# Fourier transforms of folded images in a convolution, attention and expert kernel

## The reference

```
# 1. a 7x7 depthwise convolution whose filters are computed from the image itself
g = group_norm(x)
key = softmax(K_w @ g + K_b)                  # over the 256 positions, 49 keys
filters = relu(norm(conv0_w @ (g @ key) + conv0_b) * ln_w + ln_b)
x = x + depthwise_conv(g, conv1_w @ filters + conv1_b, padding=3)
# 2. attention over the 256 positions, as tokens of 128 features
z = norm(x);  q = tanh(z);  x = x + softmax(q q^T / sqrt(128)) z
# 3. 8 experts, the best 2 for each token
z = norm(x);  p, i = top2(softmax(z @ router_w + router_b))
x = x + sum_k p_k * expert_{i_k}(z)
```

## Time and profile before

| | us |
|---|---|
| runs, median (of 3) | 386.15 (382.89 to 387.73) |
| profiled execution | 386.41 |
| its span | 384.6 |
| TensorE busy in it | 302.8 |
| VectorE busy in it | 236.7 |
| ScalarE busy in it | 132.4 |
| GpSimd busy in it | 164.2 |

### The profile page before, as it was taken

The page is one execution under the profiler, slowest core; times in us unless marked ns, Lnnn a source line. Parts: engine busy times, 40 slices in busy tenths (PEclk is TensorE's granted clock), DMA queues, the critical chain, the costliest instruction groups (busy, mean ns, idle before and its releaser), DMA issues.

```text
span 384.6 us, 7449 instructions
## 1 busy us (share of the span) xinstructions
PE 302.8 (79%) x1731; PEld 239.7 (62%) x1732; DVE 236.7 (62%) x1006; ACT 132.4 (34%) x443; POOL 164.2 (43%) x187
## 2 busy tenths in 40 slices
PE   1686989998989899998876661599999999999200
PEld 1264667786868777777664440388878787888100
DVE  2433475488887877676866652266666676666164
ACT  0312221425152515141303012266656565666000
POOL 3000010030256565555455577046656566666400
PEclk9958896999999999989887655599999999999755
DMA  7722241221523000101010013223332322231197
GB/s 221 250 80 67 84 125 28 85 68 30 182 79 97 31 30 21 38 21 37 22 35 29 29 56 107 55 80 81 85 94 84 89 77 83 80 93 59 48 322 288
DMA packets 29945, 33.37 MB, mean 87 GB/s; under 512 B 5096, under 2 KB 23740, under 8 KB 29658
## 3 DMA queue, kind: packets, MB, share of 16 engines
q1 hardware_dynamic: 23312, 22.00, 18.9%
q0 software_dynamic: 4384, 8.60, 6.7%
q10 hardware_dynamic: 2218, 2.42, 1.8%
HBM read 21.76 MB, written 11.75 MB: 87 GB/s over the span
## 4 chain that ended last, share of the span: by engine, by line
PE 44%; issue 21%; POOL 21%; DMA 5%; DVE 4%; SPq 3%; ACT 1%; POOLq 0%; DVEq 0%; ACTq 0%
POOL rows_dram L410 15%; PE bank L1324 8%; PE bank L1312 5%; PE bank L1307 5%; PE bank L1308 5%; PE bank L1317 4%; PE bank L833 3%; DMA w_high<-moe_dram 2%; PE bank L876 2%; POOL ln_rstd L437 2%; PE bank L1302 2%; SPq L1160 2%; PE bank L978 2%; POOL ln_rstd L433 2%; PE bank L914 1%
## 5 line engine op out<-in xcount | busy, mean ns | idle before, releaser
L1132 POOL DMA_INDIRECT moe_dram<-ys,xs x72 | 70.4, 978 | 51.2 <-issue 30.8
L410 POOL DMA_INDIRECT rows_dram<-row,slot x64 | 62.7, 979 | 18.2 <-issue 18.2
L1324 PE MATMUL bank<-w_all,gatedt 128*128 x288 | 44.1, 276 | 0.2 <-ACT gatedt L1175 0.2
L1249 DVE SCALAR_TENSOR_TENSOR ys<-b_all,xs,bank 128x128 f32<-128x128 f32 x72 | 25.0, 347 | 28.5 <-issue 27.0
L1259 DVE SCALAR_TENSOR_TENSOR gated<-bank,xs,silu 128x256 f32<-128x256 f32 x72 | 34.8, 483 | 10.2 <-ACT silu L1183 7.8
L1183 ACT ACTIVATE silu<-bank 128x256 f32<-128x256 f32 x72 | 27.6, 383 | 35.7 <-PE bank L1312 35.7
L1324 PEld LDWEIGHTS bank<-w_all,gatedt 128*128 128x128 f32 x288 | 38.0, 192 | 0.4 <-issue 0.4
L1307 PE MATMUL bank<-w_high,x_high 128*128 x72 | 35.6, 494 | 0.0
L978 PE MATMUL bank<-zhat,const 121*128 121x256 f32 (+1 forms) x128 | 31.2, 399 | 0.0
L1312 PE MATMUL bank<-w_high,x_low 128*128 x72 | 30.3, 421 | 0.7 <-issue 0.7
L423 POOL TENSOR_TENSOR frstd<-fvar,minus_half 128x2 f32<-128x2 f32 x8 | 5.7, 708 | 57.5 <-DVE fvar L703 57.5
(11 more groups left out here) (172 smaller groups left out, 593.7 us busy)
## 6 DMA issues: line engine op xcount, KB each, us to landing
xs<-rows_dram SPq DMA_DIRECT2D x72, 66.0 KB, 1.8
xc<-in_x SPq DMA_DIRECT2D x8, 256.0 KB, 2.9
wgv<-in_wg SPq DMA_DIRECT2D x8, 256.0 KB, 2.9
wgv<-in_wv SPq DMA_DIRECT2D x8, 256.0 KB, 3.4
xt<-in_xt SPq DMA_DIRECT2D x4, 512.0 KB, 4.6
xt<-moe_dram SPq DMA_DIRECT2D x8, 256.0 KB, 6.0
w_high<-moe_dram SPq DMA_DIRECT2D x8, 256.0 KB, 6.6
out<-w_high ACTq DMA_DIRECT2D x8, 256.0 KB, 5.6
```

The source lines that it names most:

```text
L410: pool.indirect_dma_start(rows_dram, bass.IndirectOffsetOnAxis(ap=slot[:, f % 2, 2 * t + k:2 * t + k + 1], axis=0), row[:, f % 2, t, k, :] ...
L1132: pool.indirect_dma_start(moe_dram, bass.IndirectOffsetOnAxis(ap=xs[:, u, C + 1:C + 2].bitcast(U32), axis=0), ys[:, u, :], None, bounds_ch ...
L1324: last = pe.matmul(bank_y[v][:, 0:C], gatedt[:, v, h * P:(h + 1) * P], w2_all[:, bass.ds(e * (2 * C) + h * C, C)], start=(h == 0), stop=(h ...
```

## The change

With the centre of the image as origin, the real part of a position's wave is the same at the position opposite (turned by half a turn, position 255 - n), and the imaginary part has the other sign. So the real parts of the spectrum need only the sum of an image's two halves, chunk 1 read backwards, and the imaginary parts only the difference. The change does this both ways:

- gfold holds the sum and the difference of chunk 0 and mirrored chunk 1 of gbuf; the transposes L890 take it. The forward transform has 4 products in place of 6 (one each for r = 0 and 1, two for r = 2).
- The product of image and key probabilities runs over positions, so kprob is folded too (and halved), into kfold.
- The inverse gives an even and an odd part: 4 products in place of 8. VectorE adds both to chunk 0's residual, and to chunk 1's the even part with + and the odd with -: three instructions in place of L746.
- Chunk 1 of each pair's tokens is therefore held backwards from here on. Its tokens come by an indirect DMA on GpSimd (`mirror_rows`, a table of indices `mirror`), one for each pair, in rounds 1 to 8, and SyncE loads only chunk 0. The output of chunk 1 is scattered by GpSimd in the same way; ScalarE stores chunk 0 only.
- filt, the filters before their transform, has 128 rows with zeros below row 49 and not 49 rows. The constants are shorter (fwd 732 to 490 columns, inv 1024 to 512).

```diff
@@ constants, fwd and inv @@
+    half = np.arange(P)
+    centre = (SIDE_IN - 1) / 2
+    angle = 2 * np.pi / SIDE * (np.outer(half // SIDE_IN - centre, u) + np.outer(half % SIDE_IN - centre, v))
...
+    fwd = np.concatenate([re[:, :WIDE], im[:, :WIDE], both(re, none), both(none, im)], 1)
...
-    inv = np.zeros((P, 4, HW))
+    inv = np.zeros((P, 4, P))
@@ SyncE @@
-                        sp.dma_start(xt[:, 2 * p - 4:2 * p - 2], a_in["xt"][:, 2 * p - 4:2 * p - 2]).then_inc(ld_xt[p % 2], 16)
+                        pairs = slice(2 * p - 4, 2 * p - 2)
+                        sp.dma_start(xt[:, pairs, 0:2], a_in["xt"][:, pairs, 0:2]).then_inc(ld_xt[p % 2], 16)
@@ GpSimd @@
+                pool.memset(filt[:, :, :], 0.0).then_inc(iota_ready, 1)
...
+                pool.iota(mirror[:, :], pattern=[[CHUNKS, PAIRS]], base=(P - 1) * PAIRS * CHUNKS + 1,
+                          channel_multiplier=-PAIRS * CHUNKS).then_inc(iota_ready, 1)
...
+                mirror_rows = a_in["xt"].rearrange("p b (h s) c -> (p b h) (s c)", h=CHUNKS)
                 for i in range(rounds):
                     n, a, b, c, d, e, f = stages(i)
+                    if a is not None:
+
+                        after(pool, ld_xm[a % 2], 16 * (a // 2))
+                        pool.indirect_dma_start(xt[:, a, 2:4, :].rearrange("p s c -> p (s c)"), None, mirror_rows,
+                                                bass.IndirectOffsetOnAxis(ap=mirror[:, a:a + 1], axis=0)).then_inc(ld_xm[a % 2], 16)
                     if f is not None:
@@ VectorE @@
                         dve.wait_ge(krec_done, a + 1)
+
+                        dve.tensor_scalar(kprob[:, :], kexp[:, :], krec[:, 0:1], 0.5, ALU.mult, ALU.mult).then_inc(kprob_done, 1)
+                        dve.wait_ge(kprob_done, a + 1)
                         after(dve, pt_psum, a)
-                        dve.tensor_scalar(kprob[:, :], kexp[:, :], krec[:, 0:1], None, ALU.mult).then_inc(kprob_done, 1)
+                        dve.tensor_tensor(kfold[:, 0, :], kprob[:, 0:P], kprob[:, HW - 1:P - 1:-1], ALU.add)
+                        dve.tensor_tensor(kfold[:, 1, :], kprob[:, 0:P], kprob[:, HW - 1:P - 1:-1], ALU.subtract).then_inc(kfold_done, 1)
...
+                        dve.wait_ge(ld_xm[c % 2], 16 * (c // 2 + 1))
+                        halves = t1[:, c % 2, :, :].rearrange("p (h s) c -> p h (s c)", h=CHUNKS)
+                        dve.tensor_tensor(halves, spread(bank_o[:, 0:2 * C], 1, CHUNKS),
+                                          xt[:, c, :, :].rearrange("p (h s) c -> p h (s c)", h=CHUNKS), ALU.add).then_inc(t1_step, 1)
+                        dve.wait_ge(t1_step, c + 1)
+                        dve.tensor_tensor(halves[:, 0, :], halves[:, 0, :], bank_o[:, 2 * C:4 * C], ALU.add)
+                        dve.tensor_tensor(halves[:, 1, :], halves[:, 1, :], bank_o[:, 2 * C:4 * C], ALU.subtract).then_inc(t1_done, 1)
...
+                        dve.wait_ge(g_done, n + 1)
+                        after(dve, gt_psum, n)
+                        near = gbuf[:, n % 2, :].rearrange("p (s n) -> p s n", s=2)[:, :, 0:P]
+                        far = gbuf[:, n % 2, :].rearrange("p (s n) -> p s n", s=2)[:, :, HW - 1:P - 1:-1]
+                        dve.tensor_tensor(gfold[:, 0, :, :], near, far, ALU.add)
+                        dve.tensor_tensor(gfold[:, 1, :, :], near, far, ALU.subtract).then_inc(gfold_done, 1)
@@ TensorE @@
-                        for h in range(CHUNKS):
+                        parts = ((r, r),) if r < 2 else ((2, 0), (3, 1))
+                        for q, h in parts:
                             last = pe.matmul(bank_s[r // 2][0:tile_rows[r], r % 2 * 2 * C:(r % 2 + 1) * 2 * C],
-                                             fwd[:, h, tile_cols[r]], gt[:, b % 2, h, :],
-                                             start=(h == 0), stop=(h == CHUNKS - 1))
+                                             fwd[:, tile_cols[q]], gt[:, b % 2, h, :],
+                                             start=(q == parts[0][0]), stop=(q == parts[-1][0]))
...
-                                             tapf[0:KK, tile_cols[r]], filt[:, :, :].rearrange("k s c -> k (s c)"),
+                                             tapf[:, tile_cols[r]], filt[:, :, :].rearrange("k s c -> k (s c)"),
...
                         for h in range(CHUNKS):
-                            for r in range(4):
-                                last = pe.matmul(bank_o[:, h * 2 * C:(h + 1) * 2 * C], inv[0:tile_rows[r], r, h * P:(h + 1) * P],
-                                                 zhat[0:tile_rows[r], r, :], start=(r == 0), stop=(r == 3))
+                            for r in (h, h + 2):
+                                last = pe.matmul(bank_o[:, h * 2 * C:(h + 1) * 2 * C], inv[0:tile_rows[r], r, :],
+                                                 zhat[0:tile_rows[r], r, :], start=(r < 2), stop=(r >= 2))
@@ the end: GpSimd and ScalarE @@
+        out_rows = out.rearrange("p b (h s) c -> (p b h) (s c)", h=CHUNKS)
+        for p in range(PAIRS):
+            pool.wait_ge(S["sum_done"], p + 1)
+            pool.indirect_dma_start(out_rows, bass.IndirectOffsetOnAxis(ap=mirror[:, p:p + 1], axis=0),
+                                    y_second[:, p, 2:4, :].rearrange("p s c -> p (s c)"), None).then_inc(S["pool_sent"], 16)
...
-            act.dma_start(out[:, p], y_second[:, p, :, :]).then_inc(S["stored"], 16)
+            act.dma_start(out[:, p, 0:2], y_second[:, p, 0:2, :]).then_inc(S["stored"], 16)
```

More of the change, by code:

```diff
@@ L91, in constants @@
     re, im = np.cos(angle), -np.sin(angle)
-    fwd = np.concatenate([re[:, :WIDE], im[:, :WIDE], both(re, im)], 1)
-    fwd = fwd.reshape(CHUNKS, P, -1).transpose(1, 0, 2).reshape(P, -1)
-    re, im = np.cos(shift), -np.sin(shift)
+    none = np.zeros_like(re)
+    fwd = np.concatenate([re[:, :WIDE], im[:, :WIDE], both(re, none), both(none, im)], 1)
+    re, im = np.cos(shift), np.sin(shift)
     tapf = np.zeros((P, 2 * WIDE + 2 * BOTH))
@@ L104, in constants @@
             "fwd": fwd, "tapf": tapf, "inv": inv.reshape(P, -1)}
-WIDTHS = {"ident": P, "group": P, "mean": P, "before": P, "fwd": CHUNKS * (2 * WIDE + BOTH),
-          "tapf": 2 * WIDE + 2 * BOTH, "inv": 4 * HW}
+WIDTHS = {"ident": P, "group": P, "mean": P, "before": P, "fwd": 2 * WIDE + 2 * BOTH,
+          "tapf": 2 * WIDE + 2 * BOTH, "inv": 4 * P}
 STARTS = dict(zip(WIDTHS, np.cumsum([0] + list(WIDTHS.values())).tolist()))
@@ L185, in build @@
         gbuf = sb("gbuf", [P, 2, PAIR_TOKENS])
+        gfold = sb("gfold", [P, 2, 2, P])
         gt = sb("gt", [P, 2, CHUNKS, 2 * C])
@@ L193, in build @@
         kprob = sb("kprob", [P, HW])
+        kfold = sb("kfold", [P, 2, P])
         pt = sb("pt", [P, CHUNKS, 2 * KKP])
@@ L769, in _ @@
                         after(dve, keys_done, n - 1)
-                        after(dve, gt_psum, n - 1)
                         for s in range(2):
@@ L960, in _ @@
                     if a is not None:
-                        pe.wait_ge(kprob_done, a + 1)
+                        pe.wait_ge(kfold_done, a + 1)
                         for h in range(CHUNKS):
-                            last = pe.transpose(bank_k[:, HW + h * P:HW + (h + 1) * P], kprob[:, h * P:(h + 1) * P], ident)
+                            last = pe.transpose(bank_k[:, HW + h * P:HW + (h + 1) * P], kfold[:, h, :], ident)
                         last.then_inc(pt_psum, 1)
@@ L1042, in expert_programs @@
     ZERO = EXPERTS * REGION
+    mirror = g["mirror"]
     TURNS = NB // U
@@ L1081, in expert_programs @@
     bank_x, bank_h, bank_g, bank_y = banks[0:2], banks[2:4], banks[4:6], banks[6:8]
-    names = ("consts triangle pads_sent zeros_sent pad_at_ready chain "
+    names = ("consts triangle pads_sent pool_sent pad_at_ready chain "
              "block_ready table_psum table_ready "
@@ L1161, in sync @@
         sp.wait_ge(S["stored"], 16 * PAIRS)
+        sp.wait_ge(S["pool_sent"], 16 * (1 + PAIRS))
     def scalar(act):
```

32 lines of the change are left out of this document (16 added, 16 removed).

## The result

The changed kernel takes 394.45 us (median of 4 runs, 393.19 to 395.43), the kernel before 384.52 on the same chip. The ratio is 1.029, 95% interval 1.022 to 1.036: slower, where I forecast 384 and no change. The profiled execution took 395.43 us, its span is 393.6. Some executions of several kernels here, of the kernel before too, run up to 3% longer at a lower granted clock; the ratios and intervals, and the medians of the experiments' table, leave them out.

What follows compares the result with a forecast made beforehand. TensorE is busiest (79%), but VectorE's waits and GpSimd's order were taken to limit what its saving buys. Profiled 386.41 us, -3.6 for the rounds, +1.0 for the tail: 383.8, rounded to 384; 8-in-10 range 377 to 392.

Steps and rivals of the forecast that it cites:

- the tail: Final output stores, half through GpSimd: last store free, slower GpSimd queue costs +1.0 us (bounds 0 and +3).
- the cover of the folds by VectorE's waits: At inverse transform and logits: VectorE's 22.8 us of waits for TensorE, partly untouchable, set against 16.5 us of added work.
- The sum of the rounds: Gains and losses of all rounds together: -3.6 us, with zero to 0.22 us a round for port conflicts.
- the walk: Round 7 followed row by row from 126.77 us, the other rounds the same way, each given a gain or loss.
- round 7: Net +0.6 us: saving lost waiting for gn_rstd from GpSimd, then image fold adds 0.78, though TensorE is 2.8 us shorter.
- What comes, on VectorE: Image fold 0.78, probabilities fold 0.5, residual sum 0.78 more: 2.1 us a round, 16.5 us over 8 pairs.
- What goes: TensorE loses 2 forward and 4 inverse products a round: 2.8 us, 22.4 us over 8 rounds.
- Rival 2: TensorE's clock falls in rounds 4 to 8 through idle time: 2.6 us a round, +13, 397 us; chance 0.14.
- The padding: Filter transform: its now full-height product was named as evidence against a clock fall.
- Rounds 0 and 1: One chain of short steps, with two image folds and one probabilities fold standing on it: +2.1 us.
- Backward reads and gathers: Folds: backward reads cost as forward ones; GpSimd: one 1.26 us gather a round, hidden in idle time.
- Rival 3: Backward reads or the final stores cost more: +4 to +8 us, 388 to 392; chance 0.12.

Runs made afterwards that it cites:

- e_act_out: Changed kernel with ScalarE storing all four tiles of a pair, no GpSimd DMA at the end, gathers kept: 389.21 us, ratio 1.012.
- h_repeat: Changed kernel, chunk 1 mirrored by the host layout, products issued again to make 6 forward and 8 inverse, all folds kept: 395.87 us, ratio 1.023.
- b_pad_again: Repeat of the kernel before with only the filter tile padded to 128 rows, 6 + 8 products, no folds: 381.66 us, ratio 0.991.
- b_cut: Kernel before with only fewer products (4 forward, 4 inverse), half of each transform left out, no folds, 49 rows: 386.38 us, ratio 0.997.
- h_again: Changed kernel with chunk 1 mirrored by the host layout, no GpSimd gathers or final scatters, measured once more: 389.96 us, ratio 1.013.
- b_cut_pad: Kernel before with 4 + 4 products, half of each transform left out, no folds, filter tile padded to 128 rows: 371.99 us (2 runs), ratio 0.967.
- e_scatter_only: Kernel before with only GpSimd scattering half of each output at the end, in plain order, transforms unfolded: 389.09 us, one counted run.

## Why the prediction was wrong

Two steps failed: the tail, and the cover of the folds by VectorE's waits.

**The tail: the step that failed outright.** "So the last store itself costs nothing." The transfers did cost nothing: the last sum came 2.8 us later, no more than the experts' last scatter (3.0). But I took the chain to end with the last store, and it ends with what each engine still does behind its last instruction. For GpSimd that is a record of 8.5 us, and it stood in the trace of before, at 359.4. Forecast +1.0, measured +6.2 in the trace and 5.2 in e_act_out.

**The sum of the rounds.** Forecast -3.6; the kernel without the tail (389.7, ratios 1.012 and 1.013) has +4.6 to +5. (The profiled executions differ by less, 2.8 us at the last sum; the kernel before's was a longer one, 386.41.) Folds and products were varied one by one at 128 rows, on several chips; the shares are ratios:

| us | no folds | all folds | folds cost |
|---|---|---|---|
| 6 + 8 products | 381.9 (0.992) | 395.9 (1.023) | 14.0 (3.1%) |
| 4 + 4 products | 372.0 (0.967) | 389.7 (1.013) | 17.7 (4.6%) |
| products save | 9.9 (2.5%) | 6.2 (1.0%) | |

So the folds cost 12 to 18 us and the products save 4 to 10, and the two pieces don't simply add. One way through the table is -2.6 for the padding (384.5 to 381.9), +14.0 for the folds, -6.2 for the products: +5.2. With the tail's 5 to 6 that is the 10 us measured. That this sum closes proves nothing, since its terms are differences of neighbours.

Of the walk, in the profiled executions: rounds 2 to 4 together came out 0.9 us longer (forecast -2.5), round 7 2.4 longer (forecast +0.6), round 10 0.9 shorter (forecast -1.9), round 9 1.9 shorter (forecast -1.3), and the others within 0.6 us of the forecast.

- *What comes, on VectorE.* 2.1 us a round, 16.5 in all, was right as work (15.1 measured) and came through whole, 12 to 18 us. The failed part is "against 22.8 us of waits": the walk let the logits' wait and the inverse's wait pay for the folds, but with the folds alone these waits stay at 22.4 us (h_repeat). The additions lie in other places. The image's fold has TensorE's transposes right behind it (7.8 us of waits after, 3.0 before); the residual's additions have the layer norm behind them. The walk followed VectorE alone and gave TensorE no wait for the fold; TensorE's next round has begun by then.
- *What goes.* 22.4 us of TensorE was right by the row, and 4 to 10 of it arrived. I had no such term by itself; the walk had TensorE's saving cover both the folds and a net -3.6.
- *The clock, taken as zero.* Rival 2 held in part. This is the stretch from 84 to 184 us (its length; busy us of PE, PEld, DVE, ACT, POOL; granted clock; DMA share; GB/s) in b_pad_again, b_cut and h_again:

```profile
84.00:184.00 100.00, 89.77 (x584) 75.27 (x583) 80.31 (x431) 35.80 (x136) 48.81 (x52) 1.00 0.17 54
```
```profile
84.00:184.00 100.00, 86.69 (x540) 69.48 (x540) 80.12 (x433) 35.06 (x132) 47.80 (x51) 0.95 0.17 56
```
```profile
84.00:184.00 100.00, 83.63 (x504) 69.37 (x504) 84.04 (x438) 34.65 (x131) 46.18 (x48) 0.90 0.16 53
```

  Over all traces the granted clock of this stretch is 0.97 to 1.00 in the 7 with all products, with or without folds, and 0.86 to 0.95 in the 13 with fewer. From the middle values, 0.98 and 0.93, I estimate 4 us of the 84 that TensorE is busy there. That is one part of the 12 to 18 us that did not arrive; the rest I can only place, not prove: VectorE and GpSimd's order, as in the walk. The rival's price, 2.6 us a round, was not far off where the clock fell, but of its five rounds it fell anew in one (round 4 had the lower clock before, too): in the changed kernel's profile round 7 shows it (2.4 us longer than before, forecast +0.6) and rounds 5 and 6 don't. Ahead of the fall in round 7 TensorE stood idle for 0.67, 0.42 and 0.77 us between small products; in rounds 5 and 6 the products of an expert's weights (L910, 1.96 us) lie there. So its condition, one piece of over a microsecond, was not the one either: the clock fell behind shorter pieces, and in b_cut_pad it held behind 1.52 us. The Trainium skill (TensorE: Matmul & The Clock Gate, HAM oscillation) has gaps between bursts bring back the half clock; round 7 agrees in kind, b_cut_pad's round 4 doesn't.
- *The padding, also taken as zero.* "It may keep the clock up" had the right sign, but the bound of -3.4 was too small: it is worth 2.6 us in the kernel before, 6.8 or more in the changed one and 11.3 in b_cut. I looked for its effect in rounds 9 and on; in the rows above it acts in rounds 3 and 4.
- *Rounds 0 and 1.* +2.1 forecast, +2.0 measured at VectorE's first instruction of round 2 (26.76 to 28.77). Rounds 5 and 6: -0.2 and -0.1 forecast, -0.4 and -0.1 measured. Round 10: -1.9 forecast, -0.9 measured. In the profiled execution rounds 2 and 3 were 3 us longer than before; e_act_out, with the same rounds, ran round 2 in 18.2 us like the kernel before, and e_scatter_only, with the unchanged ones, in 20.3, so 2 us of that come and go from execution to execution.
- *Backward reads and gathers* cost what I took. Rival 3's number, 388 to 392, lies near the result (so does rival 2's 397), but only its tail came, and by another mechanism than bandwidth.

## What to carry to other kernels

Before work is moved to GpSimd at the end of a program, read each engine's closing DRAIN and ask from where it will run then. An addition to the engine that closes the loop costs its full time wherever its reader stands right behind it, while a saving on the busier engine may come back in part as a lower clock; vary both sides apart before they are put in one sum, and see in the waits whether the one covers the other. And look at how many rows short products contract over: zeros for rows 49 to 127, four instructions of a round and not one column more, made a faster kernel than either, 381.9 us.

## What was not expected of the hardware

- GpSimd's closing DRAIN has a record of 8.3 to 8.7 us in the 19 profiles whose last GpSimd instruction is a scatter, and of 6.7 us behind a memset. From the end of that last instruction it is 6.6 us behind a memset or an experts' scatter, and 7.3 behind a scatter of the output. Those of the other engines took 0.73 us or less.
- The granted clock rose within a product group contracting over 128 rows (2.75 us) where with 49 rows it stayed at the lower level (3.77 us), with the same columns and the same start, 43.7 us. The group behind it ran at the full clock in 28 of 28 cases with 128 rows and in 1 of 12 with 49.
- GpSimd's fold of two SBUF operands held VectorE's cast of 8 columns for 0.46 us, to the fold's end; the power on 4 columns had held its neighbour for 0.22 only.
